# A softmax over 32-wide groups: one activation over 1024 columns, or 32 activations of 32 columns

## The reference

```python
# first layer, per sample; 4 heads of 32, q and k are [heads, 32, tokens]
q = softmax(q, axis=-2) * scale          # over the 32 entries of a head, for each token
k = softmax(k, axis=-1)                  # over the 1024 tokens
context = einsum('bhdn,bhen->bhde', k, v)
out = einsum('bhde,bhdn->bhen', context, q)
x = x + groupnorm(w_out @ out + b_out)
# second layer, per sample
sim = xn @ xn.T; val, idx = top_k(sim, 9)
v = val / val.sum()
out = silu(groupnorm(sum_k v * (xn @ w1)[idx])); out = silu(groupnorm(sum_k v * (out @ w2)[idx]))
x = x + out
```

## Time and profile before

| | |
|---|---|
| median of 3 runs | 823.76 us (823.62 to 823.89) |
| profiled execution | 824.58 us, span 822.7 us |
| PE busy | 717.5 us (87%) |
| DVE busy | 639.5 us (78%) |
| POOL busy | 483.9 us (59%) |
| ACT busy | 448.5 us (55%) in 674 instructions |
| granted PE clock, mean | 0.934 |

### The profile page before, as it was taken

One profiled execution on the slowest core, in us unless ns is written; L12 is line 12 of the kernel. 1 busy time (PEld: TensorE's weight loads), 2 busy tenths in 40 slices (PEclk: granted clock), 3 DMA queues, 4 the chain that ended last, 5 costly groups with the idle time before them and its releaser, 6 DMA issues. The chain is left out here.

```text
span 822.7 us, 15383 instructions
## 1 busy us (share of the span) xinstructions
PE 717.5 (87%) x4528; PEld 420.7 (51%) x4528; DVE 639.5 (78%) x1478; ACT 448.5 (55%) x674; POOL 483.9 (59%) x407
## 2 busy tenths in 40 slices
PE   3466979999999989998999989998999999988764
PEld 2343655555555545565555546555555555544421
DVE  2334788989898978887898978887898989887511
ACT  2122465756565647666565646576575656565510
POOL 0111667767676656676676756765676767766600
PEclk9655689999999999999999999999999999999976
DMA  2012121222222211312122221212221212121010
GB/s 77 1 39 51 52 53 62 56 66 65 65 65 66 52 55 40 74 51 65 52 64 64 64 65 35 71 45 56 65 51 52 64 52 66 52 52 39 2 26 13
DMA packets 33532, 43.28 MB, mean 53 GB/s; under 512 B 6432, under 2 KB 18976, under 8 KB 33472
## 3 DMA queue, kind: packets, MB, share of 16 engines
q1 hardware_dynamic: 33472, 42.63, 19.2%
HBM read 21.50 MB, written 8.52 MB: 36 GB/s over the span
## 5 line engine op out<-in xcount | busy, mean ns | idle before, releaser
L427 POOL TENSOR_TENSOR adj<-sim,rest 128x1024 f32<-128x1024 f32 x128 | 305.1, 2384 | 47.6 <-PE pT L915 31.8
L923 PE MATMUL pC<-adjT,xt 128*64 128x512 f32 x1024 | 237.1, 607 | 1.2 <-ACT xt L544 0.7
L523 ACT COPY adjT<-pT 128x512 f32<-128x512 f32 x256 | 141.4, 592 | 66.2 <-PE pT L915 65.7
L720 DVE MAX8 top<-sim 128x8 f32<-128x1024 f32 x128 | 156.2, 1220 | 4.4 <-ACT sim L512 3.4
L915 PE MATMUL pT<-cst,adj 128*128 128x128 f32 x1024 | 149.6, 285 | 11.0 <-POOL adj L427 6.8
L725 DVE MATCH_REPLACE8 rest<-top,sim 128x1024 f32<-128x1024 f32 x128 | 154.6, 1208 | 0.0
L512 ACT COPY sim<-pS 128x1024 f32<-128x1024 f32 x128 | 129.3, 1010 | 39.9 <-PE pS L901 39.9
L915 PEld LDWEIGHTS pT<-cst,adj 128*128 128x128 f32 x1024 | 121.2, 149 | 49.4 <-issue 26.1
L923 PEld LDWEIGHTS pC<-adjT,xt 128*64 128x64 f32 x1024 | 70.6, 139 | 125.6 <-issue 117.2
L897 PE MATMUL pS<-hihi,hilo 128*128 128x512 f16 x256 | 101.1, 395 | 2.7 <-ACT sim L512 2.4
L901 PE MATMUL pS<-lolo,hilo 128*128 128x512 f16 x256 | 100.5, 393 | 0.0
(11 more groups left out here) (131 smaller groups left out, 1077.5 us busy)
## 6 DMA issues: line engine op xcount, KB each, us to landing
xa<-x SPq DMA_DIRECT2D x32, 128.0 KB, 2.9
xu<-x SPq DMA_DIRECT2D x32, 128.0 KB, 2.7
x_kept<-x SPq DMA_DIRECT2D x16, 256.0 KB, 2.1
rbc<-rn_row SPq DMA_DIRECT2D x32, 128.0 KB, 2.8
hihi<-xhi SPq DMA_DIRECT2D x64, 64.0 KB, 2.0
lolo<-xlo SPq DMA_DIRECT2D x64, 64.0 KB, 2.0
x1c<-x_kept SPq DMA_DIRECT2D x16, 256.0 KB, 3.1
vbc<-v_row SPq DMA_DIRECT2D x32, 128.0 KB, 2.9
```

The costliest lines, as they stand in the source:

```text
L427: pool.tensor_tensor(adj[r % 2][:, :], sim[r % 4][:, :], rest[r % 2][:, :], ALU.subtract).then_inc(done["tile_adj"], 1)
L523: act.copy(adjT[p][:, NJ * k:NJ * (k + 1), r * P:(r + 1) * P], pT[:, k, :, :]).then_inc(done["half_adjT"], 1)
L720: dve.max(top[:, r, :], sim[r % 4][:, :]).then_inc(done["tile_top"], 1)
L923: mm = pe.matmul(pC[h * C:(h + 1) * C, :], xt[:, t % NJ, t // NJ, :], adjT[p][:, t, h * H:(h + 1) * H], start=(t == 0), stop=(t == NT - 1))
```

## The change

The subtraction `qs` and the sum `qsum` on DVE go. DVE's maximum is negated, and ACT runs one Exp for each of the 32 groups, straight from PSUM, with the negated maximum as bias and the sum through the accumulator into `qsum`. The 32 stand in four steps of eight, at places 422, 434, 446 and 458; each step counts q_exp up by one, and DVE's reciprocal waits for all four.

```diff
-        "attend": [248, 284, 293, 396, 422, 543, 570],
+        "attend": [248, 284, 293, 396, 422, 434, 446, 458, 543, 570],
...
-        "attend": [3, 57, 66, 107, 150, 293, 403, 433, 454, 468, 469],
+        "attend": [3, 57, 66, 107, 150, 293, 403, 454, 469],
...
-                act.wait_ge(done["q_sub"], b + 1)
+                act.wait_ge(done["q_max"], b + 1)
                 act.wait_ge(*since("q_norm", b))
-                act.activation(qe[:, :, :], qs[:, :, :], ACT.Exp).then_inc(done["q_exp"], 1)
-                yield
+                for part in range(4):
+                    for n in range(part * NT, (part + 1) * NT):
+                        e = act.activation(qe[:, n, :], pA[:, n * D:(n + 1) * D], ACT.Exp, bias=qmax[:, n:n + 1], scale=1.0,
+                                           accum_out=qsum[:, n:n + 1])
+                    e.then_inc(done["q_exp"], 1)
+                    yield
...
-                dve.tensor_reduce(qmax[:, :], q_ps, AX.X, ALU.max).then_inc(done["q_max"], 1)
-                yield
-                dve.wait_ge(done["q_max"], b + 1)
-                dve.wait_ge(*since("q_exp", b))
-                dve.tensor_tensor(qs[:, :, :], q_ps, qmax[:, :].unsqueeze(2).broadcast_to([P, NT * HEADS, D]),
-                                  ALU.subtract).then_inc(done["q_sub"], 1)
+                dve.wait_ge(*since("q_exp", 4 * b))
+                dve.tensor_reduce(qmax[:, :], q_ps, AX.X, ALU.max, negate=True).then_inc(done["q_max"], 1)
...
-                dve.wait_ge(done["q_exp"], b + 1)
-                dve.tensor_reduce(qsum[:, :], qe[:, :, :], AX.X, ALU.add).then_inc(done["q_sum"], 1)
-                yield
-                dve.wait_ge(done["q_sum"], b + 1)
+                constant_first(dve, 4 * (b + 1))
+                dve.wait_ge(done["q_exp"], 4 * (b + 1))
                 dve.wait_ge(*since("q_norm", b))
                 dve.reciprocal(qrec[:, :], qsum[:, :]).then_inc(done["q_rec"], 1)
```

More of the change, by code:

```diff
@@ L150, in build @@
         mT = sb("mT", [P, C])
-        qs = sb("qs", [P, NT * HEADS, D])
         qe = sb("qe", [P, NT * HEADS, D])
@@ L224, in build @@
             in_aggr in_mean_ps in_dev in_sq in_var_ps in_veps in_rstd y_ready k_ps k_max k_exp ek_T
-            ekT_copied yT_ps yT_copied ky_ps ky_copied k_rec m_ps m_copied q_ps q_max q_sub q_exp q_sum
+            ekT_copied yT_ps yT_copied ky_ps ky_copied k_rec m_ps m_copied q_ps q_max q_exp
             q_rec q_norm q_T qh_copied att_ps att_copied att_stat att_aggr att_mean_ps att_dev att_sq
```

## The result

| | before | after |
|---|---|---|
| median | 823.69 us (822.72 to 823.89, 4 runs) | 926.52 us (925.51 to 927.49, 4 runs) |
| profiled execution, span | 824.58, 822.7 | 925.65, 923.6 |
| ACT busy, instructions | 448.5 (55%), 674 | 571.5 (62%), 1682 |
| DVE busy | 639.5 (78%) | 613.8 (66%) |
| PE busy, mean clock | 717.5 (87%), 0.934 | 750.2 (81%), 0.926 |

The ratio is 1.1251, 95% interval [1.1231, 1.127]: slower by 103 us, where 94 were forecast.

What follows compares the result with a forecast made beforehand. Each engine works off one fixed order, so the late qrec was taken to delay VectorE's queue and the g2 mean: 6.1 + 6.1 + 4.8 + 13 x 5.92 = 94.0 us, giving 918 us; range 890 to 975.

Steps and rivals of the forecast that it cites:

- The pair: ScalarE: one 32-column ACTIVATE and its accumulator read take 0.273 us of the queue; 32 pairs take 8.74 us.
- Rival A: ScalarE: the read holds up the next ACTIVATE, 0.37 us a pair, +50 us, 968 us; chance 0.18.
- The 0.31 us: ScalarE: a pair by the Trainium skill's figures, making the sum about 19 us longer; the measured row was preferred.
- The path: Last exponential, qrec, VectorE's queue, g, g2 mean on TensorE: the longest of three paths, +5.92 us a steady sample.
- TensorE's wait: TensorE, free at 421.04, idles 3.2 us a sample for the first adjT copy, which ends at 424.1.
- VectorE's removed work: qs and qsum, 2.41 us a sample ahead of qrec: credited with nothing, becoming idle time; busy time down by 38 us.
- rival B: TensorE's clock falls after the new idle time: 0.3 to 1.7 us a sample, 922 to 940 us; chance 0.14.
- The signs: Trace checks: forecast wrong if the sample pitch grows clearly less than 5.9 us, or clearly more with pairs 0.27 us apart.
- The first three samples: Filling: the first two samples cost +6.1 us each, the third +4.8 us.
- Rival C: Something gives back: only the 4.5 us path through qn remains, 899 us, or cheap pairs, about 872; chance 0.15.
- Rival D: Faster than before: VectorE's 2.4 us arrive, needing at most 0.09 us a pair; say 805 us; chance 0.03.
- a pair of 0.25 us: ScalarE: lower end of the forecast's pair range 0.25 to 0.31 us, given as 910 to 938 us; chance 0.48.

Runs made afterwards that it cites:

- e3: Changed kernel with the 32 activations but without the accumulator, VectorE's sum back ahead of qrec; 897.88 us, ratio 1.0921.
- e1: Changed kernel with the two adjT copies put ahead of the pairs in ScalarE's order; 938.02 us, ratio 1.1409.
- e6: Changed kernel with sim's tile 7 ahead of tile 3's transposes on TensorE and qrec just ahead of g on VectorE; 903.01 us, ratio 1.0975.
- e8: Changed kernel with 8 activations of 128 columns, each over four groups, in place of 32 of 32 columns; 840.77 us, ratio 1.0219.
- e4: Kernel before without qs and qsum, exponential straight from PSUM, reciprocal taken of the maxima; 817.72 us, ratio 0.9934.
- e9: Changed kernel with 8 activations of 128 columns and xhi moved behind all four parts in ScalarE's order; 852.5 us, ratio 1.0342.
- e10: Kernel before without the maximum and the subtraction, sum kept, exponential straight from PSUM; 808.57 us, ratio 0.981.
- e11: Changed kernel with eleven half-precision products that nobody reads in TensorE's wait ahead of tile 3's transposes; 934.2 us, ratio 1.1333.
- experiment 8: Kernel before with three small VectorE operations a sample done once ahead of the loop; 827.67 us, ratio 1.0062.

## Why the prediction was right

**The pair** was predicted at 0.273 us and is 0.264; the read's share, 0.09 from the earlier trace rows, is 0.094 (e3). Rival A, a read that holds up the next ACTIVATE, did not happen: an accumulating ACTIVATE starts 0.09 to 0.10 us after the start of the read before it. The 0.31 us that the prediction worked out from the Trainium skill, "ScalarE: Activation LUTs", section "What ACT_TABLE_LOAD costs", are too high here.

**The path.** qrec moved by 10.74 - 4.90 = 5.84 us against 5.92 forecast. Behind it qrec to g takes 4.51 us (4.52 before), g to the mean 2.08 (2.07). That VectorE's queue behind qrec is the last path and TensorE's wait for adjT only accompanies it, e1 shows (wait taken away, slower) and e6 too (less work between qrec and g, 23 us faster). TensorE's wait was forecast at 3.2 us and is 3.03.

**VectorE's removed work, credited with nothing.** Right, with one thing missed: its busy time fell by 25.7 us and not by 38, since xn grew from 1364 to 2181 ns in the mean, 13.1 us over 16, beside GpSimd. That is also why its idle time ahead of qrec is 7.1 us and not 8.3. It lies in VectorE's new slack and cost nothing in this kernel; in e8, where the slack is small, it delays every sample by 0.84 us.

**Where the sum was off.** The last qrec is 101.9 us later (790.27 for 688.35), where 94.0 were forecast; each part below is read from the starts of xt2, qrec, the mean and the attention product in both traces.
The clock was rival B's 0.3 to 1.7 us a sample and not in the sum. It is 0.62 in a straight sample of the loop (1.96 us from the mean to the attention product, for 1.34), 1.1 in the first sample with a turn, nothing in the other three, and 0 to 0.9 in the rest: 5.0 us in all. With it a straight sample grew by 5.84 + 0.62 = 6.46 us. The signs named a pitch that grows by clearly more than 5.9 us; this 0.5 is the clock.
The turns of the loop, which the working did not have at all, grew by 7.7 us beyond the late qrec (the four took 222.4 us in place of 190.2; 4 x 5.84 and 1.1 of the clock are counted elsewhere). Why they grew was not tested.
The first three samples took 13.7 us for 17.0. The third's own shift is 4.69 us, from kyT (110.32) to qrec (120.70), and was forecast at 4.8. But of the 12.43 us that the first two had cost (5.94 and 6.49) only 8.99 reached its kyT: the filling before it, where the engines still have gaps, took up 3.4, and the working let it take up nothing.
The rest, 1.5 us, is the shift itself, 5.84 in the loop for 5.92, and 0.7 behind the third sample. 94.0 + 5.0 + 7.7 - 3.3 - 1.5 = 101.9. So 12.7 us that were missing stand against 4.8 that were too many: that the total is off by only 8 us is partly luck.

**Rival C** (something gives back) did not come behind qrec: qrec to g takes 4.51 us as before, and what gave back lies in the filling. **Rival D** needed 0.09 us a pair, a third of what it is. Two statements were wrong arithmetic. ScalarE was to rise to 70 to 80%: 448.5 + 16 x (8.74 - 1.06) = 571.4 us is 62% of 918. 571.5 was measured, but that it fits so well is luck, since the measured pairs give 448.5 + 16 x (8.43 - 1.06) = 566.4; the records of the copies beside them are longer (sim 1.12 us for 0.99). And a pair of 0.25 us would give 906 us, not 910; nothing hangs on it.

## What to carry to other kernels

Cost a batch of tiny instructions by their start-to-start pitch in the same form (here 0.17 us for 32 columns, 0.264 with the read), not by recorded durations, and compare it with the slack of the one instruction that waits for the batch. The slack of the consumer decides, not the engine's share: ScalarE was 55% busy, but of the 8.43 us of pairs only 2.6 fit ahead of qrec's old start (4.90 us after xt2's, less the 0.48 until the first pair, 1.41 for sim and xhi, and 0.42 from the last pair to qrec), and the other 5.84 went into the time, sample after sample. Where two in-order queues meet at one instruction, moving one of them alone only moves the wait; and work taken from a busy engine is worth what its followers can use, which may be nothing.

## What the runs showed of the hardware

**VectorE beside GpSimd.** xn and xlo, VectorE TENSOR_TENSORs of 128x512 with both inputs in SBUF, end 0.53 to 0.56 us after the GpSimd TENSOR_TENSOR during which they start, in each of the six traces that were gone through for it (before, after, e4, e8, e9, e10): xn takes 0.68 us alone and 2.46 to 2.51 beside most of adj (e8: adj ends 469.54, xn 470.09; e9: 474.55 and 475.10), xlo 0.63 and 2.14 to 2.35 beside qn. Once in e4 and once in e10 it also hit y, a tensor_scalar with one SBUF input, 0.28 us behind adj's end:

```profile
255.94 2.34 POOL L425 TENSOR_TENSOR adj<-sim,rest 128x1024 f32<-128x1024 f32 x1 [0.17 <-POOL rest L421]
256.04 2.52 DVE L624 TENSOR_SCALAR y<-xa,st_in 128x512 f32<-128x512 f32 x1 [0.28 <-issue]
```

MAX8 and MATCH_REPLACE8 (1.22 and 1.21 us), the BATCH_NORM_STATS2 (0.69) and g, whose one input is in PSUM (0.68), never changed. The Trainium skill, "SBUF — State Buffer", section "Who interferes with whom", has one port pair shared by the two engines, an exclusive lock, which a VectorE instruction with two SBUF inputs needs and one with a single SBUF input does not, outside the modes with two ports. The rows of xn, xlo and g agree; whether y ran in such a mode no run shows.

**What half clock costs depends on where it falls.** The slow stretch came after a stretch with TensorE busy 1.97 of 5 us, lasted about 6.8 us, and cost 0.62 us, since most of it lay under another engine's path. With the gap filled (e11) it came later and cost 1.1.

**The loop's turns** took 2.4 to 4.3 us more than a straight sample each before, 5.4 after, and nothing more after the first in e4 and e10; at the one of 2.4 us the clock stayed at 1.00. The cause is open (experiment 8).
